# Projection steps 4 to 27 as engine loops, expert pieces in four transfers, the rest of the routing ahead of the loop

## What is computed

```python
xn = _layernorm(x, axis=-1)
Q = lif(layer_norm(query @ Wq.T + bq, gq, betaq), 1.0)     # query is xn; K and V alike
attn = Dh - hamming + log_pe_bias(N, N)[None, None]
out = lif(jnp.einsum('bhlm,bhmd->bhld', attn * scale, V), 0.5)
...
logits = jnp.einsum('nh,eh->ne', xt, router_w)
scores, expert_idx = jax.lax.top_k(jax.nn.softmax(logits, axis=-1), TOP_K)
h = jnp.einsum('nh,ehd->end', xt, up_proj)
hidden = jax.nn.silu(h[..., :D]) * h[..., D:]
out_e = jnp.einsum('end,edh->enh', hidden, down_proj)
...
x = x + attention(xn) + experts(xn)
```

## Time and profile before

| | us |
|---|---|
| median of 3 timed runs | 441.24 |
| lowest, highest | 440.59, 441.71 |
| span of the profiled execution | 510.6 |
| PE busy in it | 384.5 |
| POOL busy in it | 211.0 |

### The profile page before, as it was taken

How to read it: one execution, slowest core, us unless ns; L and a number is a source line. 1 busy time by engine, 2 the same in 40 slices (tenths; PEclk the granted TensorE clock), 3 DMA queues, 4 the chain that set the end, 5 groups by cost and what they waited for, 6 DMA issues and landing times.

```text
span 510.6 us, 9171 instructions
## 1 busy us (share of the span) xinstructions
PE 384.5 (75%) x2517; PEld 312.9 (61%) x2526; DVE 273.3 (54%) x774; ACT 232.6 (46%) x752; POOL 211.0 (41%) x213
## 2 busy tenths in 40 slices
PE   5498773110113999998999999999999999999960
PEld 2234662100112999997778888888888887667650
DVE  5799971000100687996545444554455442458995
ACT  1567421000001788986545544454445543366650
POOL 5242467777771000000233333333333333259993
PEclk9799985555555799999999999999999999999995
DMA  8721223222220111320443344343443332495222
GB/s 269 247 96 41 83 83 125 104 104 104 104 105 31 42 41 41 106 83 1 144 131 121 121 119 136 118 124 113 124 134 123 118 98 74 184 369 193 100 84 83
DMA packets 40432, 58.98 MB, mean 116 GB/s; under 512 B 6294, under 2 KB 27926, under 8 KB 40408
## 3 DMA queue, kind: packets, MB, share of 16 engines
q1 hardware_dynamic: 31712, 38.53, 24.5%
q0 software_dynamic: 6848, 18.70, 10.1%
q10 hardware_dynamic: 1848, 1.47, 0.9%
HBM read 35.79 MB, written 22.89 MB: 115 GB/s over the span
## 4 chain that ended last, share of the span: by engine, by line
PE 54%; issue 21%; DVE 10%; POOL 7%; DMA 3%; ACT 2%; SPq 1%; POOLq 0%; DVEq 0%; ACTq 0%
PE bank L1108 15%; PE bank L1109 14%; PE bank L1110 14%; POOL xres L718 3%; PE bank L1186 3%; PE bank L1251 3%; POOL xres L711 3%; PE bank L1235 3%; DMA xn<-x 2%; DVE xn L787 2%; DVE xst L765 2%; POOL rstd L703 1%; DVE w_f L808 1%; PE bank L1174 1%; PE bank L1195 1%
## 5 line engine op out<-in xcount | busy, mean ns | idle before, releaser
L692 POOL DMA_INDIRECT slot_y<-ey,dest x71 | 68.5, 965 | 214.6 <-ACT ey L554 186.2
L500 ACT ACTIVATE junk<-bank 128x256 bf16<-128x256 f32 x96 | 35.7, 379 | 89.8 <-remote 71.7
L677 POOL DMA_INDIRECT slot_x<-xn,pos x64 | 61.6, 963 | 23.9 <-issue 19.2
L996 DVE TENSOR_TENSOR hid<-gact,bank 128x256 f32<-128x256 f32 x71 | 29.9, 421 | 76.6 <-ACT gact L538 51.0
L1108 PE MATMUL bank<-ew,exT_h 128*128 x142 | 62.6, 441 | 5.6 <-issue 4.3
L1110 PE MATMUL bank<-w_h,xT_l 128*128 128x256 f32 x192 | 56.9, 296 | 11.3 <-issue 11.2
L795 DVE TENSOR_TENSOR xT_l<-xT,xT_h 128x256 fp32r<-128x256 f32 x28 | 12.9, 460 | 98.1 <-issue 54.1
L1109 PE MATMUL bank<-w_l,xT_h 128*128 128x256 f32 x192 | 56.9, 296 | 11.2 <-issue 11.2
L1108 PE MATMUL bank<-w_h,xT_h 128*128 128x256 f32 x192 | 57.1, 297 | 10.5 <-issue 10.4
L538 ACT ACTIVATE gact<-bank 128x256 f32<-128x256 f32 x71 | 27.4, 386 | 63.8 <-PE bank L1110 63.8
L1110 PE MATMUL bank<-ew,exT_l 128*128 x142 | 55.9, 394 | 0.0
(11 more groups left out here) (193 smaller groups left out, 967.9 us busy)
## 6 DMA issues: line engine op xcount, KB each, us to landing
ex<-slot_x SPq DMA_DIRECT2D x71, 129.0 KB
y_tok<-slot_y SPq DMA_DIRECT2D x8, 1024.0 KB, 13.6
ew_f<-experts SPq DMA_DIRECT2D x24, 256.0 KB, 2.6
xres<-x SPq DMA_DIRECT2D x16, 256.0 KB, 2.8
out<-xres SPq DMA_DIRECT2D x16, 256.0 KB, 2.1
xn<-x SPq DMA_DIRECT2D x6, 512.0 KB, 11.7
slot_y<-ey,dest POOLq DMA_INDIRECT x71, 2.8
xn<-x SPq DMA_DIRECT2D x4, 256.0 KB, 3.8
```

The lines of the kernel that those rows point to most:

```text
L500: nc.scalar.activation(junk[:, i, :], proj_ps[r][i], ACT.Square, accum_out=ssq[:, r, i:i + 1]).then_inc(s["ssq_done"], 1)
L677: pool.indirect_dma_start(slot_x, bass.IndirectOffsetOnAxis(ap=pos[:, k, t:t + 1], axis=0), xn[:, t, :], None).then_inc(s["scattered"], 16)
L692: pool.indirect_dma_start(slot_y, bass.IndirectOffsetOnAxis(ap=dest[:, m % 4:m % 4 + 1], axis=0), ey[:, m % 4, :], None).then_inc(y_out[m ...
L996: v.tensor_tensor(hid[:, m % 2, :], gact[:, m % 2, :], h_ps[m % 2][:, F:2 * F], ALU.mult).then_inc(s["hid_done"], 1)
```

## The change

The float pieces are loaded straight into the place of their low part in `ew` (the tensor `ew_f` now lies over `ew`), in four transfers of 8, 10, 4 and 2 pieces, each with its own semaphore. For that the weights, the router's tensors, the biases and the pad rows move into the places of later pieces, and the transfers of those pieces wait for them; `xT` moves to one tensor under `v_spk` and `qT`. Steps 4 to 27 become loops: six passes on PE, and three passes and three passes on ACT and DVE. On DVE `rest_of_routing` stands ahead of the loop, on PE `open_kv`. Pieces 8 to 19 are split at every second step of the loops, pieces 20 to 23 in steps 28 to 31. ACT's wait at step 11 goes.

```diff
-POOL_PIECES, PIECE_STEP = 8, 5
-LOOP = 12
-LGT_PIECE, BIAS_PIECE, PAD_PIECE, XT_PIECE = 9, 13, 15, 17
-XT_TILES = NT - RG
+POOL_PIECES = 8
+PEEL, ROUND = 4, 4
+KV_OPEN = 2
+PIECE_SETS = [(0, 8), (8, 18), (18, 22), (22, PIECES)]
+WEIGHT_PIECE, LGT_PIECE, BIAS_PIECE, ROUTE_PIECE, PAD_PIECE = 8, 12, 16, 18, 22
+PIECE_ROUNDS = [(4, 16, 8), (16, 28, 14)]
+LAST_STEPS = 28
+LAST_PIECES = 20
...
-
-
-        lgT = place_in(r_w + LGT_PIECE * 2 * PW * 4)("lgT", [E, NT * P])
...
-        xT = place_in(r_w + XT_PIECE * 2 * PW * 4)("xT", [P, XT_TILES, KC, P])
...
-        r_v = ends[r_w]
-        v_spk = place_in(r_v)("v_spk", [P, NB * B * D], BF16)
-        put = place_in(r_v)
+        ew_f = place_in(r_w)("ew_f", [P, PIECES, 2, PW])
+
+        def piece_at(n):
+            return r_w + n * 2 * PW * 4
+
+        put = place_in(piece_at(WEIGHT_PIECE))
         w_f = put("w_f", [P, KC, G4 * D])
...
-        xT_v_at = r_v + XT_TILES * D * 2
-        assert ends[r_v] == r_v + NT * D * 2
-        xT_v = place_in(xT_v_at)("xT_v", [P, RG // 2, KC, P])
...
-        def steps(eng, body):
-
-
-            for t in range(8):
-                body(t, t, None)
-            with eng.Fori(0, LOOP // 4) as i:
-                for u in range(4):
-                    body(i * 4 + (8 + u), 8 + u, i)
-
-        def last_steps(body):
-            for t in range(8 + LOOP, NT):
-                body(t, t, None)
-
-        def xT_part(t):
-
-            if t < XT_TILES:
-                return xT, t
-            return (xT_v, t - XT_TILES) if t < XT_TILES + RG // 2 else (xT_q, t - XT_TILES - RG // 2)
+        def steps(eng, first, last, body):
+
+            with eng.Fori(0, (last - first) // ROUND) as i:
+                for u in range(ROUND):
+                    body(i * ROUND + (first + u), first + u, i)
...
-        def late_piece(m, i):
-
-
-            if m < 8 + LOOP and m % 2 == 0:
-                return None
-            n = POOL_PIECES + (m - PIECE_STEP) // 2 if m < 8 + LOOP else POOL_PIECES + (8 + LOOP - PIECE_STEP) // 2 + m - 8 - LOOP + 1
-            return (n + (0 if i is None else i * 2), n) if m >= PIECE_STEP and n < PIECES else None
...
-            def load_piece(n, u):
-                if not early(n, 2):
-                    sp.wait_ge(s["pool_piece"], n - 1)
-                sp.dma_start(ew_f[:, u, :], entry(pieces, n)).then_inc(piece_in[u], 16)
-
-            loop(sp, POOL_PIECES + 2, 2, lambda n, m: load_piece(n, m % 2), peel=4)
-            for n in range(POOL_PIECES + 2, PIECES):
-                sp.wait_ge(s["piece_l"], n - 1 - POOL_PIECES)
-                sp.dma_start(ew_f[:, n % 2, :], pieces[:, n]).then_inc(piece_in[n % 2], 16)
+            def load_pieces(c):
+                lo, hi = PIECE_SETS[c]
+                sp.dma_start(ew_f[:, lo:hi, 1, :], pieces[:, lo:hi, :]).then_inc(piece_in[c], 16)
+
+            load_pieces(0)
+            sp.wait_ge(s["routed"], 1)
+            sp.wait_ge(s["xn_done"], NT)
+            sp.wait_ge(s["w_parted"], KC)
+            sp.wait_ge(s["wo_parted"], 1)
+            sp.wait_ge(s["bias_set"], 1)
+            load_pieces(1)
+            sp.wait_ge(s["pads_placed"], 1)
+            load_pieces(2)
+            sp.wait_ge(s["pads_done"], 16 * PC)
+            load_pieces(3)
 
...
             sp.wait_ge(s["scattered"], 16 * TOPK * NT)
-            sp.wait_ge(s["pads_done"], 16 * PC)
-            sp.wait_ge(s["piece_l"], PIECES - POOL_PIECES)
             for j in range(8):
                 load_tile(j, j % 4)
             sp.wait_ge(s["spk_done"], G3 * NT)
...
@@ -476,7 +453,9 @@
                     act.wait_ge(s["xT_ready"], 1)
                     keep_xh(0)
                 if 2 <= g < 6:
-                    piece_upper(g - 2, g - 2)
+                    if g == 2:
+                        act.wait_ge(piece_in[0], 16)
+                    piece_upper(g - 2)
             halve_weights(1)
...
-            def project(t, m, i):
+            def project(t, m, n):
                 if not early(t, 4):
                     keep_qT(t - 4, m - 4)
                 if not (num(t) and t >= NT - 1):
                     keep_xh(t + 1, m + 1)
-                late = late_piece(m, i)
-                if m == 11:
-                    act.wait_ge(s["bias_set"], 1)
-                    act.wait_ge(s["pads_done"], 16 * PC)
-                if late:
-                    piece_upper(late[0], late[1], i)
+                if n is not None:
...
                 if early(t, 4):
-                    for n in ((4, 5), (), (6, 7), ())[t]:
-                        piece_upper(n, n)
+                    for k in ((4, 5), (), (6, 7), ())[t]:
+                        piece_upper(k)
                 squares(t, m)
                 if m % 2 == 1:
                     deviations(t, m)
 
             act.wait_ge(s["eps_set"], 1)
             act.wait_ge(s["xT_ready"], NT // 2)
-            steps(act, project)
-            last_steps(project)
+            for t in range(PEEL):
+                project(t, t, None)
+            for r, (lo, hi, n) in enumerate(PIECE_ROUNDS):
+                act.wait_ge(piece_in[1 + r], 16)
+                steps(act, lo, hi, lambda t, m, i: project(t, m, i * 2 + (n + (m - lo) // 2) if m % 2 else None))
+            act.wait_ge(piece_in[3], 16)
+            for t in range(LAST_STEPS, NT):
+                project(t, t, LAST_PIECES + t - LAST_STEPS)
...
-            def later_project(t, m, i):
-                if not early(t, 4):
-                    project(t, m, i)
-                if m == 4:
-                    rest_of_routing()
-
-            steps(dve, later_project)
-            last_steps(project)
+            rest_of_routing()
+            for lo, hi, n in PIECE_ROUNDS:
+                steps(dve, lo, hi, lambda t, m, i: project(t, m, i, i * 2 + (n + (m - lo) // 2) if m % 2 else None))
+            for t in range(LAST_STEPS, NT):
+                project(t, t, None, LAST_PIECES + t - LAST_STEPS)
...
                 for c in range(B * KC):
-                    mm(kv_ps[:, c * P:(c + 1) * P], far_v[:, 0:P], id_b[:, :], start=(c == 0), stop=False, skip_group_check=True)
+                    last = mm(kv_ps[:, c * P:(c + 1) * P], far_v[:, 0:P], id_b[:, :], start=(c == 0), stop=False, skip_group_check=True)
+                last.then_inc(s["kv_done"], KV_OPEN)
 
...
-                if m == 4:
-                    open_kv()
...
             pe.wait_ge(s["small_in"], 48)
-            steps(pe, project_and_sum)
-            last_steps(project_and_sum)
+            for t in range(PEEL):
+                project_and_sum(t, t, None)
+            open_kv()
+            steps(pe, PEEL, LAST_STEPS, project_and_sum)
+            for t in range(LAST_STEPS, NT):
+                project_and_sum(t, t, None)
```

More of the change, by code:

```diff
@@ L159, in spiking_moe @@
         second_row = put("second_row", [2, 2])
-        xT_v_at = r_v + XT_TILES * D * 2
-        assert ends[r_v] == r_v + NT * D * 2
-        xT_v = place_in(xT_v_at)("xT_v", [P, RG // 2, KC, P])
-        r_q = ends[r_v]
-        qT = place_in(r_q)("qT", [P, NT, KC * P], BF16)
-        xT_q = place_in(r_q + XT_TILES * D * 2)("xT_q", [P, RG // 2, KC, P])
-        put = place_in(r_q)
+        assert ends[piece_at(WEIGHT_PIECE)] <= piece_at(LGT_PIECE)
+        lgT = place_in(piece_at(LGT_PIECE))("lgT", [E, NT * P])
+        put = place_in(piece_at(BIAS_PIECE))
+        bias_f = put("bias_f", [2, G4 * D])
+        bias_h = put("bias_h", [2, G4 * D], F32R)
+        put = place_in(piece_at(ROUTE_PIECE))
         lg2, work, first, second = (put(n, [P, NT, E]) for n in ("lg2", "work", "first", "second"))
@@ L179, in spiking_moe @@
         rc = put("rc", [P, route_const.shape[1]])
-        r_a = max(ends[r_q], ends[r_v])
+        assert ends[piece_at(ROUTE_PIECE)] <= piece_at(PAD_PIECE)
+        put = place_in(piece_at(PAD_PIECE))
+        pad_rows = put("pad_rows", [P, PC, ROW])
+        w_rt = put("w_rt", [P, KC, E])
+        assert ends[piece_at(PAD_PIECE)] <= piece_at(PIECES)
+        put = place_in(r_w)
+        y_tok = put("y_tok", [P, NB, B, TOPK, D])
+        spk = put("spk", [P, NB, B, D])
+        r_v = ends[r_w]
+        xT = place_in(r_v)("xT", [P, KC, NT, P])
+        v_spk = place_in(r_v)("v_spk", [P, NB * B * D], BF16)
+        r_q = r_v + NT * P * 4
+        qT = place_in(r_q)("qT", [P, NT, KC * P], BF16)
+        r_a = ends[r_v]
         put = place_in(r_a)
@@ L184, in spiking_moe @@
         w_l = put("w_l", [P, KC, G3 * D], F32R)
-        r_e = r_a + 2 * KC * G3 * D * 4
-        ew_f = put("ew_f", [P, 2, PW])
+        r_e = ends[r_a]
         ex = place_in(r_e)("ex", [P, 4, ROW])
@@ L247, in spiking_moe @@
         x_in = [sem(f"x_in{c}") for c in range(len(X_CHUNKS))]
-        piece_in = [sem(f"piece_in{i}") for i in range(2)]
+        piece_in = [sem(f"piece_in{i}") for i in range(len(PIECE_SETS))]
         ex_in = [sem(f"ex_in{i}") for i in range(4)]
@@ L972, in project @@
                     spikes(t - 3, m - 3, 1)
-                late = late_piece(m, i)
```

(13 more changed lines are left out.)

57 lines of the change are left out of this document (20 added, 37 removed).

## The result

The changed kernel takes 443.43 us (median of 18 runs, 442.06 to 444.79) beside 439.92 us for the kernel before (18 runs, 438.25 to 442.25): ratio 1.0076, 95% interval 1.0059 to 1.0092. It is 3.5 us slower.

The account below looks back on a forecast made before the run. The prediction took the scatter, from `pos` to the first expert tile, to bound the kernel. Terms 0 + 0 + 0 + 2.6, of which 2.4 was kept, gave 441.24 + 2.4 = 443.6 us, range 437.5 to 446.

Parts of the forecast that it names:

- The likeliest case: Joined transfer of pieces 0 to 7 delays xrstd: DVE's last xn tiles +1.6, overlap +1.0, pos +2.6; 442.6 to 445, chance 0.53.
- the 1.07 us gap of DVE: Ahead of DVE's last eight xn tiles: idle covering piece 1's POOL subtraction; losing that cover adds 1.0 us.
- My 150: PE's projections in the kernel before, without the stall, end at about 150 us, 10 us before the first expert tile.
- The low clock after the wait: PE idling before the first expert tile drops to half clock for 10.4 us of renewed work, 5.2 us lost.
- nearly all the stall belongs to the profiled execution: PE and ACT stall beside the scatter, 91 us of the span; 69.4 of it is not in the timed median.
- the test that I named: Profile after: if the stall is gone in the loop, reading it as unordered waiting that spares no code is wrong.
- The 2.2 us that my reading left around the span: Timed median 441.24 less the span estimated without the stall, 439.0 with the clock loss.
- POOL isn't slowed by anything; the pace is its own.: Scatter instructions issue back to back at 1.27 us an interval, 88.74 us over 70; DMA traffic beside it costs 0.
- The terms at nothing: In PE's slack: loops 0 (0.7 uncovered), moved routing 0 (up to 2.8 uncovered), ACT's pad wait 0 (5 us more slack).
- Faster: Rival: stall partly real in timed runs, 7.5 us beyond the scatter, and loops remove it; about 437.5 us, chance 0.17.
- No change: Rival: the eight pieces land by 30 us, so xrstd is hardly late; 441.2 to 442.4 us, chance 0.22.
- PE is the bound: Rival: timed scatter interval 1.13 us or less, so PE's end counts; 439.5 to 447 us, chance 0.08.

Follow-up runs that it names:

- first_two: Changed kernel with pieces 0 and 1 in a transfer of their own ahead of pieces 2 to 7; three runs: 513.37, 512.59, 513.91 us, ratios 1.0011, 1.0018, 1.0023.
- rstd_first: Changed kernel with POOL's fifth xrstd ahead of the low part of piece 0: 514.74 us, ratio 1.0042 to the kernel before.
- after_again: The changed kernel, unedited, run again as a control on a chip with the stall: 515.73 us, ratio 1.0081 to the kernel before.
- more_scatter: Changed kernel with eight more indirect DMAs after the scatter, to a tensor nobody reads, SP waiting for them too: 525.79 us, ratio 1.0278 to the kernel before.
- straight: Changed kernel with steps 4 to 27 written out on PE, ACT and DVE instead of loops: 514.49 us, ratio 1.0044 to the kernel before.
- dve_pieces_b: Changed kernel with pieces 0 and 1 in their own transfer and low parts of pieces 0 to 7 moved from POOL to DVE's loop steps: 435.83 us, ratio 0.9909.

## Why the prediction was right, and where it was not

**The sum.** Forecast 443.6, measured 443.43, against 439.92 for before: +2.4 was forecast, +3.5 came. The close agreement is partly luck: the 441.24 from which I started stands 1.3 us above the later median of the same kernel, and the term was 1.1 us too small.

**The likeliest case.** It was right in its path: late transfer, ACT, POOL's order, `xrstd`, DVE, `pos`. One transfer for eight pieces holds ACT (forecast until 32.2, measured 33.07); `xrstd` ends at 36.63 (36.1); DVE's last tiles start 2.16 us late (1.6) and take 0.98 longer (1.0); `pos` is 3.2 late (2.6). The term that was too small is the landing: I added 3.9 to 4.6 us to 28.1, the slowest landing of before, and the 2 MB transfer came at 33.0, 10.3 us after its issue; the rest follows from it. first_two took that edit back and the first scatter stood within 0.5 us of before's; rstd_first took back one of its two routes and half of the loss.

One step in it was misread: "piece 1's POOL subtraction used to fall in the 1.07 us gap of DVE". There was no gap. That subtraction already cost DVE 0.95 us in the kernel before (the tile of 1.36), and piece 0's lay beside DVE's statistics, where `xsum` took 0.88 us and not 0.17. The change doesn't add a collision; it moves them, and puts 3.94 us of idle time in DVE, of which 0.9 is made good by an earlier start of the sixteen tiles (30.06, not 30.97) and as much by the first eight running undisturbed. The two terms of the sum, 1.6 and 1.0, count only what is left of this at their place; that they match is the same difference taken at the same two points, not evidence for the gap.

And 3.2 against 3.5 is a looser match than it looks. The 3.2 is of one slow execution of after, compared with an execution on another kind of chip. In the four profiled runs that keep the joined transfer and POOL's order (after, after_again, more_scatter, straight) ACT's first high part starts between 32.06 and 33.43 and the first scatter between 67.65 and 69.18, 2 to 3.7 us late. That this path carries most of the loss is shown on chips with the stall. On the chips of the result it rests on the profile and on the bound measured there; the loops and the new layout have not been tried apart from it on such a chip.

**What bounds the timed kernel.** The scatter does, from `pos` to the first expert tile, as I had it: PE waits 14.88 us for that tile, and the runs with a longer scatter follow it one to one. My 150 was for the kernel before, 5 us of it the wait for the pads that the change takes away; for the changed kernel my terms give 145 to 148, and the projections are done at 151.2. The low clock after the wait was forecast at 10.4 us; PE's matmuls of the experts take 0.63 us each from 168.5 to 173.2 and 0.39 from 175.7, and the granted clock is 0.50 from 166.0 to 173.6 and 1.00 from 173.7. So half speed lasts 7.6 us of renewed work. From the turn of the first expert tile to the end it is 276.8 us in after and 273.8 in before, whose clock was full there: 3.0 us, where I had 5.2.

**The step that failed: "nearly all the stall belongs to the profiled execution".** It belongs to the chip. On a chip with it the timed executions hold all of it, and on one without it neither kind holds any. I compared the profile of one chip with times of another, and put the difference down to the profiler. The consequence that I drew (the timed runs have no stall) was right for the runs I was given; the reason wasn't. Nor was the test that I named: the stall is gone in the loop of after, and from this I would have concluded that the loop spares it. after_again has it in the same loop (x71), straight without a loop (x83). A profile of after alone would have misled here. The 2.2 us that my reading left around the span are about right, as a time stands 1.7 to 2.5 us above its span in the runs; but there two errors partly cancel, the clock put too high by 2.2 and the scatter, as the next paragraph has it, too short by some 4.

**"POOL isn't slowed by anything; the pace is its own."** This was read where DVE did little: nor are the first 20 intervals of before "most of them beside a working DVE", as DVE works there until 74, for seven of them. In the profile of after, with DVE busy for 61.78 us of the 88, 16 of the 70 intervals between scatters are 1.3 us or longer, up to 1.8, and the whole takes 92.8 us; in after_again, with DVE busy for 6.37, 2 of 70 are, and it takes 88.9. It isn't any work of DVE that does it: 14 of the 16 stand beside its subtraction of a piece, as here. POOL, then DVE:

```profile
108.76 0.96 POOL L658 DMA_INDIRECT slot_x<-xn,pos  x1 [0.30 <-issue]
110.03 1.08 POOL L658 DMA_INDIRECT slot_x<-xn,pos  x1 [0.30 <-issue]
111.42 1.48 POOL L658 DMA_INDIRECT slot_x<-xn,pos  x1 [0.30 <-issue]
```

```profile
111.37 0.69 DVE L918 TENSOR_TENSOR ew<-ew_f,ew  x1
```

The 28 intervals that touch such a subtraction are 1.40 us on average, the other 42 are 1.27, most of them beside DVE's spikes and `xT_l`. dve_pieces_b, with 24 of these subtractions beside the scatter in place of 16, has 21 of 70 and takes 94.0 us. The kernel before makes 16 of them too, so I take it that the same falls on both kernels and the forecast of the difference didn't suffer; no profile of before on such a chip shows it. The first expert tile is turned at 166.1 and not at about 162.6 (my 160.0 with the 2.6).

The Trainium skill (SBUF — State Buffer, Who interferes with whom) says that a DVE instruction with two inputs in SBUF contends with a POOL instruction that reads SBUF. The subtraction has two such inputs and the scatter reads `pos` there, so by that rule it is slower beside them. The trace of after agrees, and gives it a size: 4 us in 93.

**The terms at nothing.** The loops: in the profile of after the turns of the queries start, on PE:

```profile
83.29 0.28 PE L1148 MATMUL bank<-id_b,qk_spk 128*128 128x128 bf16 x2
85.99 0.28 PE L1148 MATMUL bank<-id_b,qk_spk 128*128 128x128 bf16 x2
88.90 0.28 PE L1148 MATMUL bank<-id_b,qk_spk 128*128 128x128 bf16 x2
```

2.70 a step, 2.91 over a back edge, in 14.88 us of slack: nothing, on such a chip. On a chip with the stall there is no slack: first_two, with the scatter within 0.5 us of its old start, still loses 1.1, 0.9 and 1.6 us by the medians, where I had said that three more edges would cost 0.7 without cover. How much of it is the loops wasn't separated. On that point the Trainium skill (Runtime: NRT & Kernel Launch, Instruction fetch mechanics) prefers unrolled code; straight, 1.9 us better than the loops where nothing covers them, agrees in the sign, over two chips, while q8 moved 9 packets over the whole span of after and 13 in straight. The moved routing costs PE this at step 5:

```profile
75.27 0.38 PE L1160 MATMUL bank<-bias_r,ones_r 128*128 128x256 f32 x1 [1.34 <-DVE xT_l L776]
```

1.34 of the 2.8 that I gave as the most, and covered. ACT's wait for the pads was not tried by itself; its 5 us are less than this slack.

**The rivals.** "Faster", by a stall that is real in part and that loops take away: the stall is real, but on other chips, and loops don't touch it. "No change", by eight pieces that land at 30: they land at 33. "PE is the bound": the interval is longer than 1.27 us, not shorter, and PE waits. Its 10 us of slack for the kernel before are 14.9 in the changed one.

**What stays open.** The cause of the stall. Shown is that it begins some 8 to 13 us after the first scatter, ends gradually, some 6 to 10 us after the last, holds PE (on issue) and ACT (on remote) and not POOL, moves with the scatter when that moves, and is independent of loops. That PE and ACT share something on those chips with POOL's indirect DMAs is my guess; the runs that paced POOL and could have told landed on a chip without it.

## What to carry to other kernels

One semaphore over several transfers makes the first user wait for the last byte. Split it where the first user stands ahead of the path in any queue: the loss here came through POOL's order, two engines away from the wait, and with that repaired ACT's own queue still kept half of it. Elementwise work put on POOL because it is idle isn't free while DVE is on the path; moving it behind the path gave more than the whole change had lost. An `issue` on a chain can be a lengthened instruction and no gap: look at its length before work is placed there. And before a profile is used to explain a time, look whether the two come from the same chip: repeat the unchanged kernel with a profile first.

## What was not expected of the hardware

- The same program takes 440 us on some chips and 512 us on others, by a stall of PE and ACT beside POOL's indirect DMAs. On a chip with the stall, 45 to 83 matmuls are done in 88 us; without it, 681. ACT shows it too, in after_again:

```profile
93.11 0.38 ACT L479 ACTIVATE junk<-bank 128x256 bf16<-128x256 f32 x1 [12.02 <-remote]
...
130.18 0.38 ACT L479 ACTIVATE junk<-bank 128x256 bf16<-128x256 f32 x1 [36.23 <-remote]
```

- An indirect DMA of 128 rows costs POOL 1.27 us (0.96 and 0.30 until the next) beside an idle DVE, and in after also beside most of DVE's work. Beside DVE's subtraction of a 128x512 piece it is 1.40 on average, up to 1.8.
- POOL's subtractions of a piece lengthen DVE's instructions beside them: a tile of `xn` takes 0.41 us, and up to 1.40 in the profile of after; without POOL's pieces the longest of 32 is 0.41. POOL's `xrstd` (128x8, 1.91 us) doesn't: in dve_pieces_b it runs from 30.28 beside tiles of 0.41.
